# A layer input rearranged in DRAM ahead of the merge that reads it: a two-layer edge GNN with residual and layernorm

## The chip, the cores and the metric

The kernel runs on one core of a Trainium2 chip. The metric is the device time of one execution in microseconds (us); the kernel before is given by the median of three runs. All times of single instructions come from one profiled execution.

## The reference

There are 100,000 nodes with 96 features (`x`) and 50,000 edges, sorted by destination, with 32 features each. Two convolutions follow one another, and the result is added to the input and normalised:

```python
def conv(x, src, dst, edge_attr, W_msg, W_edge, W_root, b):
    msg = x[src] @ W_msg + edge_attr @ W_edge
    agg = segment_max(msg, dst, num_segments=x.shape[0])
    agg = where(isneginf(agg), 0.0, agg)
    return agg + x @ W_root + b
c1 = leaky_relu(conv(x, ..., layer 1))
c2 = leaky_relu(conv(c1, ..., layer 2))
out = layernorm(x + c2)          # over the 96 features, eps 1e-5
```

## The kernel before, in words

The work runs as four stages, one after the other: edge phase 0, merge 0, edge phase 1, merge 1 (called the first and second edge phase and the first and second merge below). The first two make layer 1, the last two layer 2 with the residual sum and the layernorm.

**Edge phase.** It loops over 98 groups of 512 edges (the last one shorter). GpSimd gathers the source rows with four indirect DMAs per group (L397). TensorE turns edges (L443), makes messages (L450), VectorE runs a segmented maximum as a scan (L866), and TensorE turns the result back (L460) so that VectorE can keep it in `hold`. Between the groups the node rows pass through TensorE for `x @ W_root + b` (L473, L482); ScalarE copies this "root" part out (L634) and stores it to DRAM in halves of superblocks (L638). Loads are issued by SP: edge attributes (L286), keep row (L294), node blocks (L266, L272). The rings hold four edge groups and four node units.

**Merge.** The nodes are cut into 49 superblocks of 2048 rows (the last has 1696), 16 blocks of 128 each; each superblock has two halves. A superblock's table in DRAM (`root`, `nodes_1`) is in superblock order: partition p holds rows p*16 to p*16+15 of the table, so that each partition reads one contiguous run; block j of partition p is node j*128+p of the superblock. SP loads the root part of a half (L313) into one of four buffers, ScalarE seeds it into PSUM (L670), TensorE adds the maxima with a one-hot matrix per chunk and block (L570, 1172 steps), and ScalarE evacuates the half (L684). In the first merge VectorE makes the one-hots (L880) and SP stores the half to `nodes_1` (L336). In the second merge GpSimd widens one-hot bytes that were stored earlier (L412, L430), and VectorE finishes each superblock: leaky relu (L932), add `x` (L935), statistics (L937), then the small steps of the variance (L945 to L951, with ScalarE's square root at L719), and the normalisation, 13 of 16 blocks on ScalarE (L725) and three on VectorE (L955). SP stores the result (L349).

**x in the second merge.** `load_x(s)` (L319 to L331) reads superblock s of `x` straight from the input. `x` is in node order, so partition p gets 16 rows that lie 128 rows apart: 2048 runs of 384 bytes. Two buffers `x_in` alternate; the load for s waits until VectorE has added the one for s - 2.

**SP's order.** SP issues its DMAs in one order written out by hand, each behind its own wait (L353 to L378). In the first merge it takes, half by half, the store of half h (waits for the evacuation) and the root load of half h + 8 (waits for the seed of half h + 4). After that it waits for the last stores (L360 to L363) and signals `ready` (L364), for which GpSimd waits before the gathers of the second edge phase (L407). In the second edge phase it takes a group's attributes, its keep row and the node blocks that are due. Before the second merge it issues two superblocks' root loads, the first two of x, and two more superblocks' root loads; in the merge, for each s, it loads x for s + 1, root for s + 4, and stores the output of s - 1.

Of the kernel before, what the change touches and what calls it, by code (L numbers as in the profile page):

```python
# [5 lines left out]
F32 = mybir.dt.float32  # L6
# [6 lines left out]
P = 128  # L13
# [3 lines left out]
DMA = 16  # L17
# [3 lines left out]
SBN = RI * P  # L21
# [19 lines left out]
def gnn(nc, x, src, dst, edge_attr, weights, out):  # L41
    N, D = x.shape
# [6 lines left out]
    NE = EG + 1  # L49
    CH = -(-E // P)  # L50
    E_END = E - (CH - 1) * P
    NSB = -(-N // SBN)
    N_END = N - (NSB - 1) * SBN
# [15 lines left out]
    with ExitStack() as ctx:  # L69
        def sb(name, shape, dt):  # L70
            return ctx.enter_context(nc.sbuf_tensor(name, shape, dt))

        def sem(name):
            return ctx.enter_context(nc.semaphore(name))

        def sems(name, n=2):
            return [sem(f"{name}{i}") for i in range(n)]


        root = nc.dram_tensor("root", (NSB * SBN, D), F32, kind="Internal").ap()  # L80
        nodes_1 = nc.dram_tensor("nodes_1", (NSB * SBN, D), F32, kind="Internal").ap()
        keep_dram = nc.dram_tensor("keep_row", (E,), BF16, kind="Internal").ap()

        onehot_dram = nc.dram_tensor("onehot_bytes", (-(-NBATCH // 2), P, 2 * BATCH * P), U8, kind="Internal").ap()

        def table(a, s):
            return a[s * SBN:(s + 1) * SBN, :].rearrange("(p j) d -> p (j d)", j=RI)

        def unit_of(a, u):
            s, h = divmod(u, 2)  # L90
            return table(a, s)[:, h * UB * D:(h + 1) * UB * D]
# [15 lines left out]
        rows = sb("rows", [ROWS_ON + 1, TP], I32)  # L107
# [18 lines left out]
        x_in = [arena[:, UNIT_RING * UW + (3 + i) * SW:UNIT_RING * UW + (4 + i) * SW] for i in range(2)]  # L126
# [60 lines left out]
        bytes_stored, bytes_in = sems("bytes_stored"), sems("bytes_in")  # L187
        stepped, seeded, evacuated = sems("stepped"), sems("seeded"), sems("evacuated")
        root_back, nodes_stored = sems("root_back", UNIT_RING), sems("nodes_stored", 3)
        x_back, vec_2, var_done, dev_done, norm_set = sems("x_back"), sem("vec_2"), sem("var_done"), sem("dev_done"), sem("norm_set")  # L190
        norm_a, norm_v, out_stored = sem("norm_a"), sem("norm_v"), sems("out_stored", 3)


# [16 lines left out]
        def byte_batches(g):  # L210

            span = NE - BYTES_AT
            return range((g - BYTES_AT) * NBATCH // span, (g + 1 - BYTES_AT) * NBATCH // span) if g >= BYTES_AT else range(0)
# [14 lines left out]
        def unit_uses(u, layer):  # L228
            return uses(u, UNIT_RING, NU, layer)
# [2 lines left out]

        X_ADDED, X_ADD = 4, 2
        LAST_BLOCKS = -(-N_END // P)

        def scalar_blocks(s):

            return LAST_BLOCKS // 2 if s == NSB - 1 else 15 if s >= NSB - 3 else 13

# [6 lines left out]
        def _(sp):  # L246
            first = 8
            src_groups = src[0:EG * GE].rearrange("(g p r) -> p g r", p=P, r=C)
            to = src_all[:, 0:EG * C].rearrange("p (g r) -> p g r", r=C)
# [11 lines left out]
            def load_nodes(layer, u):  # L261
                if u >= UNIT_RING:
                    sp.wait_ge(nt_full, layer * NG + (u - UNIT_RING + 1) * UG)
                to = node_in[u % UNIT_RING]
                if layer:
                    sp.dma_start(to, unit_of(nodes_1, u)).then_inc(block_in[u % UNIT_RING], DMA)  # L266
                    return
                rows = U_END if u == NU - 1 else UN
                full = rows // GE
                to = to.rearrange("p (q j d) -> p q j d", j=C, d=D)  # L270
                at = x[u * UN:u * UN + full * GE, :].rearrange("(q p j) d -> p q j d", p=P, j=C)
                sp.dma_start(to[:, 0:full, :, :], at).then_inc(block_in[u % UNIT_RING], DMA)  # L272
                if rows > full * GE:
                    at = x[u * UN + full * GE:N, :].rearrange("(p j) d -> p j d", j=C)
                    sp.dma_start(to[0:(rows - full * GE) // C, full, :, :], at).then_inc(block_in[u % UNIT_RING], DMA)

            def store_bytes(k):
                sp.wait_ge(bytes_made, k + 1)
                sp.dma_start(onehot_dram[k // 2][:, k % 2 * BW:(k % 2 + 1) * BW], bytes_out[:, k % 2, :]).then_inc(bytes_stored[k % 2], DMA)

            def edge_phase(layer):
                for g in range(NE):
                    t = EdgeGroup(layer, g)
                    if t.o >= EDGE_RING:
                        sp.wait_ge(turned, max(t.o - EDGE_RING + 1, layer * NE))
                    sp.dma_start(gathered[t.ring][0:t.p, :, D:K], attr_at(t)).then_inc(attr_in[t.ring], DMA)  # L286
                    if t.o == 0:
                        sp.wait_ge(keep_made, 1)
                        sp.dma_start(keep_dram.rearrange("(p c) -> p c", c=MC), keep_all).then_inc(keep_stored, DMA)
                        sp.wait_ge(keep_stored, DMA)  # L290
                    if t.o >= EDGE_RING:
                        sp.wait_ge(scanned, t.o - EDGE_RING + 1)
                    row = keep_dram[g * GE:g * GE + t.cols].rearrange("(a e) -> a e", a=1)
                    sp.dma_start(keep[0:D, t.ring, 0:t.cols], row.broadcast_to([D, t.cols])).then_inc(keep_in[t.ring], DMA)  # L294
                    for u in unit_loads.get((layer, g), ()):
                        load_nodes(layer, u)
                    if layer == 0:
                        for k in byte_batches(g - EDGE_RING):
                            store_bytes(k)
                for u in unit_loads.get((layer, NE), ()):  # L300
                    load_nodes(layer, u)
                if layer == 0:
                    for g in range(NE - EDGE_RING, NE):
                        for k in byte_batches(g):
                            store_bytes(k)

            def load_root(layer, u):
                if u >= UNIT_RING:
                    sp.wait_ge(seeded[layer], (u - UNIT_RING + 1) * UG)
                else:  # L310
                    sp.wait_ge(nt_full, (layer + 1) * NG)
                sp.wait_ge(root_stored[u % UNIT_RING], DMA * unit_uses(u, layer))
                sp.dma_start(root_in[u % UNIT_RING], unit_of(root, u)).then_inc(root_back[u % UNIT_RING], DMA)  # L313

            def load_roots(layer, s):
                for u in (2 * s, 2 * s + 1):
                    load_root(layer, u)

            def load_x(s):  # L319
                if s >= 2:  # L320
                    sp.wait_ge(vec_2, X_ADDED * (s - 2) + X_ADD)
                else:
                    sp.wait_ge(eb_full, 2 * NE)
                    sp.wait_ge(no_full, 2 * NG)
                rows = N_END if s == NSB - 1 else SBN
                full = rows // P
                to = x_in[s % 2].rearrange("p (j d) -> p j d", d=D)
                at = x[s * SBN:s * SBN + full * P, :].rearrange("(j p) d -> p j d", p=P)
                sp.dma_start(to[:, 0:full, :], at).then_inc(x_back[s % 2], DMA)
                if rows > full * P:  # L330
                    sp.dma_start(to[0:rows - full * P, full, :], x[s * SBN + full * P:N, :]).then_inc(x_back[s % 2], DMA)  # L331

            def store_half(h):
                s, at = h // 2, slice(h % 2 * HG * C * D, (h % 2 + 1) * HG * C * D)
                sp.wait_ge(evacuated[0], (h + 1) * HG)
                sp.dma_start(table(nodes_1, s)[:, at], nodes_out[s % 3][:, at]).then_inc(nodes_stored[s % 3], DMA)  # L336
# [19 lines left out]
            for h in range(2 * NSB):  # L356
                store_half(h)
                if h + 8 < NU:
                    load_root(0, h + 8)
            for k in range(3):  # L360
                sp.wait_ge(nodes_stored[k], 2 * DMA * ((NSB + 2 - k) // 3))
            for i in range(2):
# [2 lines left out]
            edge_phase(1)  # L365
            load_roots(1, 0)
            load_roots(1, 1)
            load_x(0)
            load_x(1)
            load_roots(1, 2)  # L370
# [364 lines left out]
        def _(dve):  # L735
# [133 lines left out]
            def hold_chunks(t):  # L869
                dve.wait_ge(eb_full, t.o + 1)  # L870
                whole = sum(n == P for _, n in t.chunks)
                a = t.g * C
                last = nc.vector.tensor_copy(hold[:, a:a + whole, :], eb_ps[:, 0:whole * D].rearrange("p (c d) -> p c d", d=D))
                for c, n in t.chunks[whole:]:
                    last = nc.vector.tensor_copy(hold[0:n, a + c, :], eb_ps[0:n, c * D:(c + 1) * D])
                last.then_inc(held, 1)
# [44 lines left out]
            def finish(s):  # L921
                blocks = LAST_BLOCKS if s == NSB - 1 else RI
                y = nodes_out[s % 3][:, 0:blocks * D]
# [68 lines left out]
```

## Time and profile before

| what | value |
|---|---|
| median of three runs | 1887.03 us (1883.07 to 1889.02) |
| span of the profiled execution, first to last instruction | 1876.7 us |
| time of the profiled execution itself | not listed apart from its span; the median lies 10.3 us above the span |
| busy: TensorE matmul / VectorE / ScalarE / GpSimd | 1519.6 / 1313.2 / 1080.4 / 1084.8 us |
| moved by DMA | 459.13 MB, 245 GB/s over the span |
| chain that ended last | TensorE 30%, VectorE 25%, DMA 19%, GpSimd 15%, issue 9% |
| mean granted TensorE clock | 0.950 |

How to read it: PE is TensorE's matmul, PEld its weight load, DVE is VectorE, ACT ScalarE, POOL GpSimd, SP SyncE; "SPq" is SP's instruction queue, and q1, q10 and q0 are the DMA queues of SP, ScalarE and GpSimd. L12 is line 12 of the kernel. The DMA share is the mean busy share of the core's 16 DMA engines. In the chain, "issue" is time in which an engine waited for nothing that the profile shows. A long fp32 matmul step at L570 stands as two matmul records. The busy shares are averages over four stages with different limits, so they say little by themselves.

### The profile page before, as it was taken

To read this page: it belongs to the slowest core of one execution; us is meant where nothing else is said; L and a number is where in the kernel's file an instruction comes from. 1 tells how busy PE (TensorE), PEld (TensorE's weight loads), DVE (VectorE), ACT (ScalarE), POOL (GpSimd) and SP (SyncE) were. 2 spreads that over 40 slices of the span, in tenths; PEclk is the share of its full clock that TensorE was granted. 3 is DMA by queue.
4 is the path that set the end of the run, shared out by engine and by line. 5 is a ranking of instruction groups with operands and counts; after the bars stand their busy time and mean duration, and the time that the engine had idled before them with its cause. 6 is when DMAs were issued, how large, how long until landed. Compare 5 with 4: busy or idle time off the path is not lost.

```text
span 1876.7 us, 37108 instructions
## 1 busy us (share of the span) xinstructions
PE 1519.6 (81%) x11422; PEld 1348.9 (72%) x11422; DVE 1313.2 (70%) x2383; ACT 1080.4 (58%) x2450; POOL 1084.8 (58%) x1454
## 2 busy tenths in 40 slices
PE   3998888988889888886889888988987767676763
PEld 3677777777778888885778777777777667666662
DVE  3677676777665555553667767677736899999998
ACT  2354444545443455553555555555535888888887
POOL 6777777767600000002777777777757787675663
PEclk9999999999999999998999999999998998988887
DMA  7779999999865777885788888888867899999996
GB/s 145 203 213 266 271 266 263 264 276 273 245 226 169 226 248 261 279 277 189 204 225 228 238 229 235 226 223 242 223 223 215 267 290 298 296 299 296 294 300 176
DMA packets 505022, 459.13 MB, mean 245 GB/s; under 512 B 348553, under 2 KB 412340, under 8 KB 504836
## 3 DMA queue, kind: packets, MB, share of 16 engines
q1 hardware_dynamic: 444118, 321.15, 59.9%
q0 software_dynamic: 30976, 57.72, 12.7%
q10 hardware_dynamic: 29742, 77.88, 10.6%
q8 instruction: 103, 1.69, 0.4%
q14 instruction: 83, 0.68, 0.1%
HBM read 283.25 MB, written 173.37 MB: 243 GB/s over the span
## 4 chain that ended last, share of the span: by engine, by line
PE 30%; DVE 25%; DMA 19%; POOL 15%; issue 9%; ACT 1%; SPq 1%; POOLq 0%; DVEq 0%; ACTq 0%
PE ps L570 18%; DMA onehot_bytes<-arena 14%; POOL arena L397 13%; DVE stats L937 6%; DVE arena L880 4%; DMA arena<-nodes,src_perm 4%; DVE arena L935 4%; DVE arena L932 4%; PE ps L482 4%; POOL onehot L430 2%; PE ps L450 2%; PE ps L473 2%; PE ps L443 2%; DVE arena L955 2%; DVE arena L866 1%
## 5 line engine op out<-in xcount | busy, mean ns | idle before, releaser
L570 PE MATMUL ps<-hold,onehot 128*128 x4688 | 612.7, 293 | 186.2 <-POOL onehot L430 139.5
L570 PEld LDWEIGHTS ps<-hold,onehot 128*128 128x128 f32 x4688 | 582.3, 205 | 217.0 <-issue 216.8
L397 POOL DMA_INDIRECT arena<-nodes,src_perm x392 | 370.0, 944 | 473.4 <-SPq L364 354.2
L482 PEld LDWEIGHTS ps<-w_root,onehot 97*128 97x128 f32 x3136 | 400.9, 194 | 99.7 <-issue 97.5
L397 POOL DMA_INDIRECT arena<-in_x_dram,src_all x392 | 374.4, 955 | 143.0 <-issue 114.3
L482 PE MATMUL ps<-w_root,onehot 97*128 97x128 f32 x3136 | 417.6, 277 | 0.0
L430 POOL CAST onehot<-keep 128x256 f32<-128x256 uint8 x588 | 298.8, 556 | 115.5 <-PE ps L570 72.4
L634 ACT COPY arena<-ps 128x384 f32<-128x384 f32 x392 | 187.5, 478 | 274.2 <-PE ps L482 272.4
L684 ACT COPY arena<-ps 128x384 f32<-128x384 f32 x392 | 166.6, 477 | 208.6 <-PE ps L570 208.5
L866 DVE TENSOR_TENSOR_SCAN arena<-keep,arena,ps 96x512 f32<-96x512 bf16 x196 | 247.7, 1264 | 46.6 <-PE ps L450 46.2
L880 DVE TENSOR_TENSOR onehot<-count,rel 128x1024 f32<-128x1024 bf16 x147 | 179.5, 1222 | 142.3 <-PE ps L570 141.2
L880 DVE TENSOR_TENSOR arena<-ps,rel 128x1024 uint8<-128x1024 f32 x147 | 175.5, 1216 | 110.6 <-DMA onehot_bytes<-arena 110.4
L473 PE MATMUL ps<-ident,arena 128*96 128x128 f32 x1568 | 240.9, 277 | 0.0
L725 ACT ACTIVATE arena<-arena,small 128x96 f32<-128x96 f32 x635 | 232.7, 454 | 1.6 <-DVE small L951 1.6
L450 PE MATMUL ps<-arena,w_edge 128*96 128x512 f32 x392 | 207.2, 611 | 0.0
L443 PE MATMUL ps<-ident,arena 128*128 128x128 f32 (+1 forms) x784 | 125.7, 284 | 96.2 <-DMA arena<-nodes,src_perm 63.7
L670 ACT COPY ps<-arena 128x384 f32<-128x384 f32 x392 | 175.9, 488 | 8.8 <-DMA arena<-root 8.3
L473 PEld LDWEIGHTS ps<-ident,arena 128*96 128x96 f32 x1568 | 177.2, 128 | 2.8 <-issue 2.4
L851 DVE TENSOR_TENSOR arena<-ps,arena 128x512 f32<-128x512 f32 x98 | 67.6, 690 | 146.9 <-ACT arena L613 144.5
L443 PEld LDWEIGHTS ps<-ident,arena 128*128 128x128 f32 (+1 forms) x784 | 93.2, 146 | 106.9 <-DMA arena<-nodes,src_perm 61.4
L624 ACT COPY onehot<-ps 96x512 f32<-96x512 f32 x196 | 114.3, 583 | 95.1 <-PE ps L473 92.4
L460 PE MATMUL ps<-ident,arena 96*128 96x96 f32 (+1 forms) x782 | 99.0, 249 | 52.8 <-DVE arena L880 51.8
(97 smaller groups left out, 1158.4 us busy)
## 6 DMA issues: line engine op xcount, KB each, us to landing
root<-arena ACTq DMA_DIRECT2D x196, 384.0 KB
arena<-root SPq DMA_DIRECT2D x196, 384.0 KB, 4.4
nodes<-arena SPq DMA_DIRECT2D x98, 384.0 KB, 2.7
arena<-nodes SPq DMA_DIRECT2D x98, 384.0 KB
arena<-in_x_dram SPq DMA_DIRECT2D x97, 384.0 KB
arena<-in_x_dram SPq DMA_DIRECT2D x48, 768.0 KB, 8.0
out_dram<-arena SPq DMA_DIRECT2D x48, 768.0 KB, 4.6
onehot_bytes<-arena SPq DMA_DIRECT2D x147, 128.0 KB
```

Of the source, the lines that this page charges most:

```text
L397: nc.gpsimd.indirect_dma_start(out=gathered[t.ring][0:t.p, i, 0:D], out_offset=None, in_=table_in, in_offset=bass.IndirectOffsetOnAxis(ap= ...
L430: last = nc.gpsimd.tensor_copy(onehot[:, k % NS, i:i + PIECE, :].rearrange("p t n -> p (t n)"), bytes_back(k, 1)[:, 0, i * P:(i + PIECE) * P])
L443: last = nc.tensor.transpose(et_ps[:, r:t.cols:C], gathered[t.ring][0:t.p, r, :], ident[0:t.p, 0:t.p])
L450: nc.tensor.matmul(em_ps[t.b2][0:D, 0:t.cols], w_edge[:, t.layer, :], edges_t[t.b2][:, 0:t.cols], start=True, stop=True).then_inc(em_full, 1)
L473: last = nc.tensor.transpose(nt_ps[m % 2][0:D, to], node_in[u % UNIT_RING][:, at:at + D], ident[:])
L482: last = nc.tensor.matmul(no_ps[m % 2][:, i * P:(i + 1) * P], nodes_t[m % NODE_RING][0:D + 1, i * P:(i + 1) * P], w_root[0:D + 1, layer * ...
L570: nc.tensor.matmul(ps_bytes[:, bass.ds(place_at, SLOT)].bitcast(F32), onehot[:, k % NS, i, :], flat[:, bass.ds(chunk_at, P)], start=False, ...
L634: nc.scalar.copy(root_out[u % UNIT_RING][:, at:at + C * D].rearrange("p (j d) -> p j d", d=D), no_ps[m % 2].rearrange("p (j k) -> p j k", ...
L670: nc.scalar.copy(slot[:, n % RING, :, 0:D], root_in[u % UNIT_RING][:, at:at + C * D].rearrange("p (j d) -> p j d", d=D),).then_inc(seeded[ ...
L725: last = nc.scalar.activation(nodes_out[s % 3][:, at], nodes_out[s % 3][:, at], ACT.Identity, bias=small[:, 5 + 2 * (s % 2), j:j + 1], sca ...
L866: nc.vector.tensor_tensor_scan(msgs[t.b2][0:D, at], keep[0:D, t.ring, at], em_ps[t.b2][0:D, at], msgs[1 - t.b2][0:D, GE - 1:GE], ALU.min, ...
L880: return nc.vector.tensor_tensor(to[:, 0:n, :], row.rearrange("p (a n) -> p a n", a=1).broadcast_to([P, n, P]), rel[:, k * BATCH:k * BATCH ...
```

## The change

A new DRAM table `x_laid` holds `x` in superblock order. It is filled by DRAM to DRAM transfers (`lay_x`), 25 of them in the first merge, after every fourth half, and 24 in the second edge phase, in every fourth group; each moves one superblock of 768 KB (the last one in two pieces). All are issued by SP and count on one semaphore, `laid`; SP waits for all of it before the first load of x in the second merge. `load_x` then reads `x_laid`, 128 runs of 6144 bytes. Engine work is as before.

```diff
+        x_laid = nc.dram_tensor("x_laid", (NSB * SBN, D), F32, kind="Internal").ap()
...
+        LAY_EVERY = 4
+        LAID_FIRST = NSB - NE // LAY_EVERY
...
                     for u in unit_loads.get((layer, g), ()):
                         load_nodes(layer, u)
+                    if layer and g % LAY_EVERY == 1 and LAID_FIRST + g // LAY_EVERY < NSB:
+                        lay_x(LAID_FIRST + g // LAY_EVERY)
...
+            def lay_x(s):
+                rows = N_END if s == NSB - 1 else SBN
+                full = rows // P
+                to = table(x_laid, s).rearrange("p (j d) -> p j d", d=D)
+                at = x[s * SBN:s * SBN + full * P, :].rearrange("(j p) d -> p j d", p=P)
+                sp.dma_start(to[:, 0:full, :], at).then_inc(laid, DMA)
+                if rows > full * P:
+                    sp.dma_start(to[0:rows - full * P, full, :], x[s * SBN + full * P:N, :]).then_inc(laid, DMA)
...
             def load_x(s):
...
-                to = x_in[s % 2].rearrange("p (j d) -> p j d", d=D)
-                at = x[s * SBN:s * SBN + full * P, :].rearrange("(j p) d -> p j d", p=P)
-                sp.dma_start(to[:, 0:full, :], at).then_inc(x_back[s % 2], DMA)
+                sp.dma_start(x_in[s % 2][:, 0:full * D], table(x_laid, s)[:, 0:full * D]).then_inc(x_back[s % 2], DMA)
                 if rows > full * P:
-                    sp.dma_start(to[0:rows - full * P, full, :], x[s * SBN + full * P:N, :]).then_inc(x_back[s % 2], DMA)
+                    at = slice(full * D, (full + 1) * D)
+                    sp.dma_start(x_in[s % 2][0:rows - full * P, at], table(x_laid, s)[0:rows - full * P, at]).then_inc(x_back[s % 2], DMA)
...
                 store_half(h)
                 if h + 8 < NU:
                     load_root(0, h + 8)
+                if h % LAY_EVERY == 1 and h // LAY_EVERY < LAID_FIRST:
+                    lay_x(h // LAY_EVERY)
...
             load_roots(1, 0)
             load_roots(1, 1)
+            sp.wait_ge(laid, DMA * (NSB + (1 if N_END % P else 0)))
             load_x(0)
             load_x(1)
```

## Rows read from the trace of the kernel before

**Rows 1.** Windows by stage: busy us by engine, granted clock, DMA share, GB/s
```profile
core 0: us, PE busy (x) PEld busy (x) DVE busy (x) ACT busy (x) POOL busy (x), PEclk, DMA share, GB/s
...
549.00:871.00 322.00, 282.36 (x2344) 268.81 (x2344) 178.39 (x148) 160.61 (x389) 0.00 (x0) 0.99 0.73 239
871.00:1377.00 506.00, 440.85 (x3327) 378.84 (x3328) 350.50 (x493) 264.93 (x491) 371.16 (x394) 0.97 0.81 223
...
1500.00:1830.00 330.00, 225.91 (x1564) 214.38 (x1563) 307.76 (x974) 292.38 (x793) 227.99 (x441) 0.87 0.99 296
```

**Rows 2.** The chain of waits, 1500 to 1830 us, by line
```profile
by line: DVE stats L937 28.8%; DVE arena L935 20.3%; DVE arena L932 20.1%; DVE arena L955 7.9%; issue 5.5%; ACT small L719 3.4%; DVE small L951 3.2%; DVE small L950 2.9%; DVE small L948 2.7%; DVE small L945 2.6%; DVE small L947 2.0%; DVE sm
```

**Rows 3.** Who waited for whom, 1500 to 1830 us (us in total, times, longest)
```profile
DVE small L950 <- ACT small L719: 13.5, 36, 0.4
```

**Rows 4.** A VectorE group, 1500 to 1830 us (busy us, mean ns, idle)
```profile
L932 DVE SCALAR_TENSOR_TENSOR arena<-arena 128x1536 f32<-128x1536 f32 x37 | 68.9, 1863 | 0.0
```

**Rows 5.** The chain of waits, 560 to 840 us, by line
```profile
by line: PE ps L570 87.6%; issue 12.4%
```

**Rows 6.** Chain of waits, 900 to 1370 us, and one piece
```profile
by line: POOL arena L397 44.2%; DMA arena<-nodes,src_perm 15.8%; issue 14.9%; PE ps L482 9.5%; PE ps L450 5.1%; PE ps L473 4.8%; PE ps L443 4.1%; PE ps L460 1.8%
...
1252.58 7.55 DMA arena<-nodes,src_perm
```

**Rows 7.** Line L397 alone, 900 to 1370 us: ns, and idle before
```profile
L397 POOL DMA_INDIRECT arena<-nodes,src_perm x372: 929/944/957, 899.3 to 1362.5; - x186
...
  issue: 107.6, 353
  PE ps L443: 5.8, 19
```

**Rows 8.** Queue q10, 900 to 1370 us (packets, MB, share), and issues
```profile
q10 hardware_dynamic: 13413, 36.64, 19.7%
...
root<-arena ACTq DMA_DIRECT2D x94, 384.0 KB
```

**Rows 9.** Queue q1, 1500 to 1830 us, and issues (us to landing last)
```profile
q1 hardware_dynamic: 158751, 84.39, 86.2%
...
out_dram<-arena SPq DMA_DIRECT2D x36, 768.0 KB, 4.8
arena<-in_x_dram SPq DMA_DIRECT2D x36, 768.0 KB, 8.0
arena<-root SPq DMA_DIRECT2D x72, 384.0 KB, 6.1
```

**Rows 10.** Line L329 alone, whole span: time of SP's issue, ns min/median/max
```profile
L329 SPq DMA_DIRECT2D arena<-in_x_dram x49: 384/1874/5982, 1378.7 to 1850.4; - x49
```

**Rows 11.** Waits of ScalarE, 1377 to 1877 us
```profile
ACT ps L670 <- DMA arena<-root: 3.5, 3, 1.4
```

**Rows 12.** DMA queue q1 and the root loads, 560 to 840 us
```profile
q1 hardware_dynamic: 24473, 66.85, 73.8%
...
arena<-root SPq DMA_DIRECT2D x86, 384.0 KB, 3.6
```

**Rows 13.** Waits of ScalarE, 549 to 871 us
```profile
ACT ps L670 <- DMA arena<-root: 2.8, 3, 1.3
```

**Rows 14.** Waits of SP, 560 to 840 us
```profile
SPq L336 <- ACT arena L684: 184.1, 86, 9.7
SPq L313 <- ACT ps L670: 33.1, 85, 0.4
```

**Rows 15.** Windows of 40 us, columns as in Rows 1
```profile
560.00:600.00 40.00, 36.38 (x307) 34.70 (x306) 22.88 (x19) 13.24 (x32) 0.00 (x0) 1.00 0.45 146
...
640.00:680.00 40.00, 34.50 (x288) 32.83 (x288) 22.30 (x19) 19.85 (x48) 0.00 (x0) 1.00 0.75 239
...
760.00:800.00 40.00, 35.09 (x295) 33.42 (x295) 22.30 (x19) 23.16 (x56) 0.00 (x0) 1.00 0.87 278
```

**Rows 16.** The chain of waits, 868 to 878 us, one piece
```profile
871.66 2.29 DMA nodes<-arena
```

**Rows 17.** Waits of SP, 900 to 1370 us
```profile
SPq L294 <- DVE arena L866: 309.8, 90, 6.7
```

More of the change, by code:

```diff
@@ L189, in gnn @@
         root_back, nodes_stored = sems("root_back", UNIT_RING), sems("nodes_stored", 3)
-        x_back, vec_2, var_done, dev_done, norm_set = sems("x_back"), sem("vec_2"), sem("var_done"), sem("dev_done"), sem("norm_set")
+        x_back, laid, vec_2, var_done, dev_done, norm_set = sems("x_back"), sem("laid"), sem("vec_2"), sem("var_done"), sem("dev_done"), sem("norm_set")
         norm_a, norm_v, out_stored = sem("norm_a"), sem("norm_v"), sems("out_stored", 3)
```

## The prediction

> **What bounds the kernel now.** I read the stages first, then in each stage the chain of waits, then the DMA queues. The windows by stage [rows 1] show three that the change touches: the first merge (549 to 871 us), the second edge phase (871 to 1377) and the second merge (1377 to the end). The reader should see that the DMA engines are at 0.99 only from 1500 to 1830 us, the stage that is to read x in long runs, and that the other two stages have 0.73 and 0.81 in use.
>
> A full DMA share is not yet a bound. The chain in 1500 to 1830 us [rows 2] runs over VectorE lines (L937, L935, L932, L955) and names no transfer. VectorE is busy 307.8 of 330 us [rows 1] and its only listed wait is 13.5 us for the square root of ScalarE [rows 3]; it never waits for x. It passes L932, once per superblock and 1.86 us long, 37 times in the 330 us [rows 4]: a period of about 9.1 us. In the first merge the chain is TensorE at L570 (87.6%) and "issue" between its pieces (12.4%) [rows 5]. In the second edge phase it is mostly GpSimd's gather, 944 ns each with 0.3 us between (107.6 us over 353) [rows 6, 7]: 1.25 us each, 5.0 us for a group of four.
>
> **Prices.** A long packet: the root stores of the second edge phase are alone on q10, 94 of 128 packets of 3072 bytes in 19.7% of 16 x 470 us = 1481 us [rows 8], so 123 ns each and 0.98 us of all 16 engines for 384 KB. A short packet: q1 takes 86.2% of 16 x 330 = 4551 us [rows 9]; its 72 root loads are 72 x 128 x 0.123 = 1134 us, and 3417 us are left for 36 x loads and 36 out stores of 2048 runs of 384 bytes, 23.2 ns each, 2.97 us of all engines for 768 KB. An x load by 128 runs of 6144 bytes, at the pace of long packets, costs 2 x 0.98 = 1.96 us. So the second merge saves 1.0 us of DMA per superblock, 49 us in all.
>
> **What the second merge gains: 1 us.** VectorE's chain hides the x load before and after: a load is issued after L935 of the superblock before last, lands 8.0 us later [rows 9], and is wanted two periods (18 us) after. Nothing waits, so nothing goes. SP's issue of an x load takes 1.87 us in the median and up to 5.98 [rows 10] and will drop, but SP then waits for ScalarE anyway. At the stage's start ScalarE waits 3.5 us for root [rows 11], partly beside the first two x loads: I take -1, between -3.5 and 0.
>
> **What the lay-out costs.** 49 transfers of 2048 runs (one more small one for the tail): 25 in the first merge, one after every fourth half superblock, and 24 in the second edge phase, one in every fourth group. The trace has no DRAM to DRAM transfer. Its read half is the x load's, 2.97 us, and its write half the out store's, 2.97 us. If both overlap it costs 2.97 us of all engines, if they follow each other 5.94. No row lies nearer to one end, so I take the middle, 4.5; DMA time below nothing is excluded. The Trainium skill, in "DMA: Bandwidth & Descriptors" (Latency and other measured facts), gives 207 to 214 GB/s per direction for copies between HBM tensors with 16 KiB rows, which would make 3.7 us as an estimate from that page; the transfer would then fit more easily than at 4.5. No run here shows it.
>
> Out stores write runs of 384 bytes to DRAM and land in 4.8 us, where x loads reading such runs need 8.0 [rows 9]: the short write is not the slow side. Against that the Trainium skill says, in "DMA: Bandwidth & Descriptors" (Specifications), that transfers under 512 bytes lose line rate through a read-modify-write. By that rule the write half would be the dear one and the price nearer the upper end; the landing times don't bear it out.
>
> *First merge.* Its 98 stores and 98 root loads need 196 x 0.98 = 192 us of the 322, though the share is 0.73, 235 us: packets are stretched there (q1 has 73.8% of 16 x 280 us = 3306 us for 86 root loads and as many stores, 22,016 long packets, 150 ns per packet instead of 123 [rows 12]). With 25 lay-outs the need is 192 + 74, 112 or 149 = 266, 304 or 341 us, so it fits at the middle price. Latency: root for a half is loaded four halves ahead, 4 x 322/98 = 13.1 us; less about 2 us until seeding frees the buffer and 3.6 us of landing [rows 12], 7.5 us are left, and a lay-out ahead in the same queue takes at most 5.94. Root waits are 2.8 us now [rows 13]; I take +1, up to +4. SP waits 184.1 + 33.1 of 280 us here [rows 14], so an issue of 0.4 to 6 us is covered, though it pushes the following store and root load back inside the same slack.
> TensorE's own pace: x307 matmuls in 40 us at DMA share 0.45, x288 at 0.75 and x295 at 0.87 [rows 15]. For 2344 matmuls that is 305 against 318 us: 12 us for 0.42 more share if it is a slope, nothing if it has levelled off, as the two later windows say. The share would rise by 0.23 to 0.46. I take +4, between 0 and +13.
>
> *Between the stages.* The last lay-out (h = 97) is issued between the last store and the signal "ready", for which GpSimd's gathers wait. The store lands in 2.29 us [rows 16]; an issue of 1.87 us hides under it, one of 5.98 adds 3.7. Then the first edge and node loads stand behind a lay-out. Taken: +0.5, up to +3.7.
>
> *Second edge phase.* 410 us busy + 71, 108 or 143 = 481, 518 or 553 of 506. Again the busy time contains stretched packets, so I expect it to fit. GpSimd's pace needs no transfer: a ring of four groups is 20 us; less 5 us of its own issue, 7.5 us of landing (row at 1252.58 [rows 6]) and about 1 us of turning, 6 us are free, and a lay-out delays by 4.5 in the middle. GpSimd waits 5.8 us for the ring now [rows 7]. Key rows, edge attributes and node blocks are loaded three to four groups ahead, and SP has 309.8 us of waiting there [rows 17]. If this cover fails TensorE starves group by group. I take +2, from 0 to +8. The new wait on "laid" stands before load_x(0); behind it are load_x(1) and root loads 4 to 7, for which ScalarE would wait. The last lay-out is issued at group 93, some 20 us before, so it costs 0.
>
> **Sum:** -1 + 1 + 4 + 0.5 + 2 = +6.5 us. The profiled execution has a span of 1876.7 us, 10.3 below the median of 1887.0; its own whole time is not listed, so I carry the difference over unchanged: 1893.5.
>
> **The rivals.** (1) *All hidden.* TensorE's pace has levelled off and every queue has its slack: 1886 to 1888. For it: the last two windows of [rows 15], and GpSimd's fixed 1.25 us. Chance 0.18. (2) *The DMA engines become the bound* where there was room. If stretched packets are real need, the middle price overruns both stages: 235 + 112 - 322 = 25 and 518 - 506 = 12, 1924 in all; at the upper price 62 + 47, 1996. It decides from 3.5 us per lay-out on in the first merge (87/25). Against it: packets of the same size take 123 ns on q10, and at share 0.99 nobody waits for x. 0.15. (3) *Faster:* the full DMA share does hold the second merge, through VectorE. Of 330 us there, 307.8 + 13.5 are work and the square root; only 8.7 can go, x 49/36 = 12 us, and 3.5 at the start, less some 4 for the lay-outs: 1876. It decides if those 8.7 us are late transfers; against it, the chain puts 5.5% (18 us) on "issue" between dependent instructions [rows 2], which no transfer shortens. 0.10. (4) *The long runs are not there:* the loads of the laid-out table still go as short packets, or SP's issue stays long. Then the costs stay and the -1 goes: 1894.5. 0.07.
>
> **How the numbers follow.** The forecast, a small loss of 2 to 15 us, has 0.50. A measurement of this kernel can tell about 0.3%, 5.7 us. Over that: 0.30 of the forecast's 0.50, rival 2, 0.05 of rival 4: 0.50. Within: 0.20 of the forecast, 0.15 of rival 1, 0.02 of rival 4: 0.37. Faster: rival 3 and 0.03 of rival 1: 0.13. The range goes from 1880, which takes in rival 1 and part of 3, to 1932, which takes in rival 2 at the middle price; about 0.15 stays outside.
>
> **What would show it.** In the profile after, windows of 0.9 to 1.0 DMA share in the first merge and edge phase and about 0.88 from 1500 to 1830; the second merge's length within 3 us of 500; packets under 512 bytes halved there and more by 100,000 (49 x 2048) before it; matmuls at L570 in pieces 4.4 to 4.5 us apart; ScalarE's wait on root in the first merge under 7 us. The forecast is wrong if VectorE's periods shrink below 9.0 us, if L397 waits for TensorE by tens of us, or if L670 waits for root by more than 15 us. Landing of the lay-outs, 8 us or 16, tells the price.

## The result and the profile after

The changed kernel takes 1898.07 us in the median of five runs (1893.4 to 1904.15), the kernel before 1887.03 in five beside it (1879.45 to 1889.02); the ratio is 1.0066, 95% interval 1.0042 to 1.0089. It is slower, by 11.0 us in the medians and 12.5 by the ratio. A second comparison of the same kernel gave 1.0087 (1.0053 to 1.0121): 1900.1 against 1881.57 us, 18.5 us in the medians and 16.4 by the ratio.

For the changed kernel both the time of the profiled execution (1896.51 us) and its span (1894.7 us) are known: 1.8 us lie around the span, not the 10.3 us that I had carried over. By the same 1.8 us the profiled execution of before took about 1878.5 us, an estimate, and was quicker than each of the five beside it. So the two traces differ by 18.0 us, more than the medians do, and a part of what they show is scatter between executions. The second profile and those of the experiments tell which part.

The stages of the changed kernel, in the windows view (columns as in [rows 1]):

```profile
550.00:883.00 333.00, 285.88 (x2343) 273.09 (x2344) 177.89 (x146) 160.30 (x387) 0.00 (x0) 0.98 0.88 287
883.00:1390.00 507.00, 439.65 (x3332) 378.68 (x3332) 350.17 (x493) 265.36 (x491) 371.19 (x394) 0.97 0.92 262
...
1512.00:1842.00 330.00, 226.30 (x1568) 214.43 (x1568) 303.26 (x958) 290.19 (x787) 236.00 (x436) 0.88 0.90 294
```

The DMA share rose from 0.73 to 0.88 and from 0.81 to 0.92 in the two stages that now lay x out, and fell from 0.99 to 0.90 in the one that reads it. VectorE is as good as fully busy there as before (303.3 against 307.8 of 330 us): the relief bought nothing. By stage, in us, from the start times of the instructions at L570, L397 and L932 of before and their successors (a superblock counts as finished when VectorE starts its last steps at L932):

| profile | first merge, first to last matmul | second edge phase, first to last gather | second merge, finished superblock 1 to 13 | 13 to 41 |
|---|---|---|---|---|
| before | 321.5 | 488.2 | 130.3 | 256.5 |
| changed | 333.5 | 488.2 | 132.3 | 259.8 |
| changed, second profile | 340.8 | 488.2 | 138.3 | 255.3 |

About two thirds of what the traces differ by is in the first merge (12.0 of 18.0 us, and 19.3 of 27.8 in the second profile); the second edge phase carries its 24 lay-outs for nothing.

**Where the first merge loses.** Windows of 40 us of the changed kernel; set against [rows 15] (x307, x288, x295 matmuls in 40 us):

```profile
560.00:600.00 40.00, 36.36 (x307) 34.69 (x306) 22.46 (x20) 13.25 (x32) 0.00 (x0) 1.00 0.59 181
...
680.00:720.00 40.00, 34.17 (x288) 32.50 (x286) 22.72 (x19) 21.53 (x52) 0.00 (x0) 1.00 0.97 322
...
760.00:800.00 40.00, 33.38 (x268) 31.90 (x268) 20.12 (x18) 21.53 (x52) 0.00 (x0) 0.96 0.95 315
800.00:840.00 40.00, 33.37 (x271) 32.07 (x270) 20.63 (x17) 21.53 (x52) 0.00 (x0) 0.96 0.96 315
```

At a DMA share of 0.97 TensorE kept its old pace (x288, as before from 680 to 720 us); at 0.95 it lost 9% (x268 where it was x295). The share is not what decides. The chain of waits of the changed kernel, 808 to 834 us (start, us, what), shows the loss itself:

```profile
812.90 3.85 PE ps L586 x32
...
816.84 1.24 DVE onehot L896
818.08 1.03 issue
819.11 9.04 PE ps L586 x64
828.14 0.60 issue
828.75 3.83 PE ps L586 x32
```

TensorE stands still from 816.75 to 819.11 us. The chain names VectorE's one-hots, but those that TensorE needs next had been made at 816.3. What it waits for is its own load of the next sixteen step words (the places in the merge, read from SBUF into registers once per two batches), which runs from 815.7 to 818.9 us. From the timeline and from line L570 alone (PEldq is TensorE's instruction queue):

```profile
815.05 1.23 DVE L896 TENSOR_TENSOR onehot<-count,rel 128x1024 f32<-128x1024 bf16 x1 [1.68 <-PE ps L586]
```

```profile
L570 PEldq TENSOR_LOAD <-rows x1: 3206/3206/3206, 815.7 to 815.7; - x1
```

All such loads of the first merge (ns min/median/max), before and then changed:

```profile
L554 PEldq TENSOR_LOAD <-rows x73: 862/1268/1870, 552.1 to 868.5; - x73
```

```profile
L570 PEldq TENSOR_LOAD <-rows x73: 862/1194/4308, 553.0 to 881.1; - x73
```

The median is no worse, the longest goes from 1.87 to 4.31 us. Added up over the merge (74 with the first one, which starts before it), the loads take 96.8 us before and 105.3 after, 8.5 more; five of them last over 2 us (3.05, 2.47, 3.28, 3.21 and 4.31). All five overlap lay-out packets, where 27 of all 74 loads do. TensorE's gaps between matmuls (those over 150 ns) grow by as much, from 39.0 to 47.1 us. SP's queue shows in the timeline what stood around the load of 815.7 us, a lay-out and a store whose issue was held for 2.89 us:

```profile
811.44 0.55 SPq L329 DMA_DIRECT2D x_laid<-in_x_dram  x1
...
812.57 2.89 SPq L349 DMA_DIRECT2D nodes<-arena  x1
```

The second part is TensorE's clock. Windows of the changed kernel before and after the gap:

```profile
809.00:816.70 7.70, 6.84 (x60) 6.50 (x58) 3.83 (x4) 4.97 (x12) 0.00 (x0) 1.00 1.03 321
819.00:828.00 9.00, 8.89 (x64) 8.85 (x64) 3.67 (x3) 4.97 (x12) 0.00 (x0) 0.81 0.75 249
```

Having stood for 2.4 us, TensorE works part of the next 9 us at the lower of its two levels (granted clock 0.81 where it was 1.00): 64 matmuls take 9.04 us, where two pieces of 32 take 7.66. This happens after three gaps (2.5, 2.4 and 3.6 us; pieces at 794.23, 819.11, 859.26), 1.38 us each, and not after one of 2.3 us (720.68). In the second profile it follows four of six gaps of 2.6 to 3.2 us, so not every such stop costs it. 8.5 + 3 x 1.38 = 12.6 us, against 12.0 measured for the stage.

What I had feared did not come. ScalarE's waits for root, 2.8 us before [rows 13], and q1 with its root loads (us to landing last) in the changed kernel's first merge:

```profile
ACT ps L686 <- DMA arena<-root: 2.5, 3, 1.0
```

```profile
q1 hardware_dynamic: 67915, 83.64, 88.7%
...
arena<-root SPq DMA_DIRECT2D x86, 384.0 KB, 4.4
```

**The second merge** (1512 to 1842 us), to be set against [rows 9] and [rows 3]: q1 fell from 86.2% to 77.9%, x lands in 7.0 instead of 8.0 us, and VectorE's only listed wait is still the one for ScalarE's square root. That wait grew from 13.5 to 18.2 us (longest 3.0), which is more than the 3.3 us that the steady part of the stage lost in this profile.

```profile
q1 hardware_dynamic: 87815, 83.61, 77.9%
...
arena<-x_laid SPq DMA_DIRECT2D x36, 768.0 KB, 7.0
```

```profile
DVE small L966 <- ACT small L735: 18.2, 35, 3.0
```

### The profile page after: what moved, and what is told of

Read it like the earlier page. It is cut to its first block, busy times and chain, and to the rows that moved or that the text cites. A ratio compares the mean times of both kernels' runs of the same rounds, so it can differ in the third digit from the quotient of the medians.

```text
span 1894.7 us, 37158 instructions
## 1 busy us (share of the span) xinstructions
PE 1526.6 (81%) x11422; PEld 1359.2 (72%) x11422; DVE 1310.3 (69%) x2383; ACT 1081.1 (57%) x2450; POOL 1091.4 (58%) x1454
## 4 chain that ended last, share of the span: by engine, by line
PE 31%; DVE 20%; DMA 19%; POOL 18%; issue 10%; SPq 1%; ACT 1%; DVEq 0%; ACTq 0%; POOLq 0%
PE ps L586 20%; POOL arena L413 14%; DMA onehot_bytes<-arena 13%; DVE stats L953 4%; POOL onehot L446 4%; DVE arena L896 4%; DMA arena<-nodes,src_perm 4%; PE ps L498 4%; DVE arena L951 3%; DVE arena L948 3%; PE ps L489 2%; PE ps L466 2%; PE ps L459 1%; DVE arena L882 1%; DVE arena L971 1%
## 5 line engine op out<-in xcount | busy, mean ns | idle before, releaser
L586 PE MATMUL ps<-hold,onehot 128*128 x4688 | 622.4, 296 | 193.8 <-POOL onehot L446 135.9
L586 PEld LDWEIGHTS ps<-hold,onehot 128*128 128x128 f32 x4688 | 592.2, 208 | 224.2 <-issue 224.0
L446 POOL CAST onehot<-keep 128x256 f32<-128x256 uint8 x588 | 305.1, 569 | 114.2 <-PE ps L586 75.6
```

The source lines that it names most:

```text
L446: last = nc.gpsimd.tensor_copy(onehot[:, k % NS, i:i + PIECE, :].rearrange("p t n -> p (t n)"), bytes_back(k, 1)[:, 0, i * P:(i + PIECE) * P])
L586: nc.tensor.matmul(ps_bytes[:, bass.ds(place_at, SLOT)].bitcast(F32), onehot[:, k % NS, i, :], flat[:, bass.ds(chunk_at, P)], start=False, ...
```

## The experiments

Theory A: the loss is in the first merge, where lay-outs hold up TensorE's loads of step words and the clock falls after the long gaps; the rest is scatter. Rivals put part of it into the second merge (B), into chance (C), or held that full DMA engines do bound something (D). Stage times in us, one profile each, as in the table above:

| run | ratio, 95% interval | first merge | second edge phase | superblocks 1 to 13 | 13 to 41 |
|---|---|---|---|---|---|
| lay_merge_only | 1.0094 (1.0062 to 1.0126) | 341.5 | 488.1 | 131.0 | 258.1 |
| lay_edge_only | 1.0013 (0.9993 to 1.0033) | 322.4 | 488.2 | 130.8 | 256.0 |
| long_runs_only | 1.0017 (0.999 to 1.0045) | 321.3 | 489.2 | 139.7 | 256.1 |
| lay_both_edges | 1.0434 (1.0405 to 1.0462) | 323.3 | 489.1 | 141.6 | 256.3 |
| lay_halves | 1.0039 (1.0019 to 1.0059) | 326.6 | 488.2 | 130.1 | 256.2 |
| lay_merge_act | 1.0078 (1.0051 to 1.0104) | 332.8 | 488.2 | 128.6 | 255.6 |
| lay_both_edges_act | 1.0282 (1.0252 to 1.0312) | 321.7 | 488.1 | 135.1 | 255.8 |
| words4 | 1.0464 (1.0433 to 1.0495) | 362.7 | 488.9 | 148.8 | 287.1 |
| long_runs_3072 | 1.0001 (0.9985 to 1.0018) | 322.3 | 488.5 | 129.7 | 257.6 |
| lay_second_edge_all | 1.0015 (0.999 to 1.0041) | 321.4 | 488.6 | 130.2 | 259.5 |
| lay_merge_double | 1.0185 (1.0154 to 1.0215) | 355.1 | 488.2 | 130.8 | 256.2 |
| changed_again | 1.0087 (1.0053 to 1.0121) | 340.8 | 488.2 | 138.3 | 255.3 |

### The parts one by one

**Lay-outs in the first merge alone** (against the changed kernel):

```diff
-                    if layer and g % LAY_EVERY == 1 and LAID_FIRST + g // LAY_EVERY < NSB:
-                        lay_x(LAID_FIRST + g // LAY_EVERY)
...
-                sp.dma_start(x_in[s % 2][:, 0:full * D], table(x_laid, s)[:, 0:full * D]).then_inc(x_back[s % 2], DMA)
+                sp.dma_start(to[:, 0:full, :], at).then_inc(x_back[s % 2], DMA)
```

> The 25 lay-outs of the first merge stay, the 24 of the second edge phase are left out, and x is read from the input in short runs as before. Theory A (the loss is in the first merge: TensorE's loads of step words are held up by the lay-outs, and its clock falls after the long gaps): first merge about 333 us instead of 321, the rest as before, ratio to the kernel before 1.005 to 1.007. Rival B (part of the loss is in the second merge, where the traces differ by 6 us, because of the long runs): ratio 1.002 to 1.004. Rival C (the two profiled executions differ mostly by chance): ratio within 1.002.

These 25 lay-outs carry the whole loss and more, beyond the 333 us and the 1.007 that theory A had named: first merge 341.5 us, ten step-word loads over 2 us, all ten beside lay-out packets (31 of the 74 loads are). B and C fall as explanations of the whole.

**Lay-outs in the second edge phase alone** (the same with `lay_x` left out of the first merge instead):

> The 24 lay-outs of the second edge phase stay, those of the first merge are left out, and x is read from the input as before. Theory A: the gathers set the pace, so the second edge phase stays at 488 us from first to last gather and the ratio is 0.999 to 1.001. A rival by which DMA load costs wherever it stands: +6 us or more, ratio over 1.003.

As theory A has it: 488.2 us, and a ratio that can't be told from 1.

**Long runs alone**:

```diff
+                if s < NSB - 1:
+                    sp.dma_start(x_in[s % 2][:, 0:full * D], table(x, s)[:, 0:full * D]).then_inc(x_back[s % 2], DMA)
+                    return
```

> No lay-outs; the second merge reads x by runs of 6144 bytes straight from the input (all superblocks but the last), so the residual adds x rows in the wrong order. This is the change's gain without its cost. Theory A: VectorE's chain hides the loads, second merge unchanged within 2 us, DMA share 0.90 instead of 0.99, ratio 0.998 to 1.001. Rival B: slower by about 6 us, ratio 1.003. Rival D (the full DMA share did hold the second merge): faster by 8 us or more, ratio under 0.996.

No gain: D falls. B's ratio of 1.003 lies inside the interval, so a small loss by the long runs is not excluded. The steady part of the second merge is untouched (256.1 us), but superblocks 1 to 13 took 139.7 us instead of 130.3, which theory A had not said and B had; see the runs of 3072 bytes below.

### All lay-outs in the edge phases

```diff
-                if h % LAY_EVERY == 1 and h // LAY_EVERY < LAID_FIRST:
-                    lay_x(h // LAY_EVERY)
...
-                    if layer and g % LAY_EVERY == 1 and LAID_FIRST + g // LAY_EVERY < NSB:
-                        lay_x(LAID_FIRST + g // LAY_EVERY)
+                    if g % LAY_EVERY == 1 and (LAID_FIRST + g // LAY_EVERY < NSB if layer else g // LAY_EVERY < LAID_FIRST):
+                        lay_x(LAID_FIRST * layer + g // LAY_EVERY)
```

> The 25 lay-outs move from the first merge into the first edge phase, one in every fourth group; everything else is as in the changed kernel. Theory A: the first merge returns to 321 us; the first edge phase already has a DMA share of 0.86 and TensorE waits there on VectorE's bytes, so it pays between 0 and 6 us; ratio 0.999 to 1.003. If the cost of a lay-out follows from the DMA share alone, the first edge phase, fuller than the first merge, pays 12 us or more: ratio over 1.006.

I was far off: the first merge is back at 323 us, but it begins at 625.3 us instead of 549.1. The first edge phase lost 76 us, over six times the 12 of the rival. The waits of this kernel, 20 to 620 us, and line L282 alone, the byte stores (ns of SP's issue, min/median/max):

```profile
DVE arena L894 <- DMA onehot_bytes<-arena: 146.2, 52, 6.8
...
PE ps L474 <- DVE arena L894: 98.2, 32, 6.3
```

```profile
L282 SPq DMA_DIRECT2D onehot_bytes<-arena x147: 319/320/5244, 114.4 to 619.1; - x147
```

There a loop is closed over a transfer: VectorE makes one-hot bytes into two buffers, waits until the store of the last but one has landed (110.4 us in all before, 146.2 now), and TensorE waits for VectorE (51.8 us before, 98.2 now). A lay-out ahead of the store in SP's queue can lengthen a round. Part of the 76 us is TensorE's clock: from 20 us to just before the merge (620 us here, 540 before) its granted clock is 0.90 where it was 0.98, and its busy time 490 us where it was 456. With the 25 lay-outs of that phase issued by ScalarE, in its own edge phase after its root stores:

```diff
+                    if layer == 0 and g % LAY_EVERY == 1:
+                        lay_x(g // LAY_EVERY)
```

> As the run with all lay-outs in the two edge phases, which lost 76 us in the first one, but ScalarE issues the 25 of the first edge phase (q10). Theory Q: the 76 us come from VectorE's byte stores standing behind lay-outs in SP's queue (VectorE waits for a store with only two buffers); in another queue the stores pass, and the first edge phase falls from 625 to 550 to 570 us, ratio 1.000 to 1.012. Theory L (DMA load as such): it stays at 600 us or more, ratio over 1.03.

It begins the merge at 592.6 us: 33 of the 76 us went with the place in the queue, 43 stay. VectorE's waits for the byte stores are 131.6 us and TensorE's for VectorE 73.5, still above those of before, and the granted clock is 0.94. That the rest comes from stores sharing the engines with lay-outs is likely, not shown. The truth lies between both theories, and nearer to L than I thought.

### What makes the step-word loads long

**The grain.** Each lay-out cut in two, issued after every second half:

```diff
+                js = slice(c * RI // 2, (c + 1) * RI // 2)
+                sp.dma_start(to[:, js, :], at[:, js, :]).then_inc(laid, DMA)
...
-                if h % LAY_EVERY == 1 and h // LAY_EVERY < LAID_FIRST:
+                if h % 2 == 1 and h // 2 < 2 * LAID_FIRST - 1:
```

> As the run with lay-outs in the first merge alone (first merge 341.5 us, ratio 1.009), but each lay-out is cut into two of 1024 runs, issued after every second half; the same bytes and as many packets. Theory A1 (a step-word load of TensorE is late because it falls into a long burst of lay-out packets and the backlog behind it): bursts are half as long, no load over 2.5 us, first merge 321 to 328 us, ratio under 1.004. Theory A2 (the amount of DMA work decides, not its grain): first merge 335 to 345 us as with whole lay-outs, ratio 1.007 to 1.012.

A1: two loads over 2 us instead of ten, the longest 2.32, and 326.6 us instead of 341.5, for nearly the same bytes (49 halves instead of 50) at a higher DMA share (0.91 instead of 0.86 from 560 to 850 us). The intervals of the two ratios do not touch.

**The queue.** The lay-outs issued by ScalarE after every fourth half:

```diff
                     reseed(2 * s + 1)
+                    if layer == 0 and s % 2 == 0:
+                        lay_x(s // 2)
```

> As the run with lay-outs in the first merge alone, but ScalarE issues them, so they stand in q10 and not ahead of SP's stores and root loads in q1. If the long step-word loads come from the backlog in SP's queue: none over 2 us, first merge near 322 us. If from the DMA engines being full, whichever queue fills them: 335 to 345 us, as before. ScalarE's own issue costs 0.6 us each, hidden by its waits on TensorE.

332.8 us, short of the 335 to 345 of the second theory but far from 322. In this kernel's profile eleven loads last over 2 us, none over 2.44 (line of the load, ns min/median/max):

```profile
L559 PEldq TENSOR_LOAD <-rows x74: 846/1331/2441, 551.3 to 884.3; - x74
```

This fits loads of 3 to 4 us by the backlog in SP's queue and those just over 2 by the filled engines, but one run that also moves the lay-outs in time does not show it; and seven of its gaps, 10.2 us, ended with VectorE's one-hots and not with the load. This run also gives a lay-out's price, since in 560 to 850 us the lay-outs are alone in q10:

```profile
q10 hardware_dynamic: 43293, 16.50, 21.2%
...
x_laid<-in_x_dram ACTq DMA_DIRECT2D x21, 768.0 KB, 7.8
```

21.2% of 16 x 290 us = 984 us over 21 x 2048 packets is 22.9 ns each, 2.93 us of all engines per superblock: the lower end of my range, as the landing after 7.8 us says too. Reading and writing overlap, and 384-byte runs at both ends in DRAM cost what they cost at one end (23.2 ns). 786,432 bytes in 2.93 us of engine time would be 268 GB/s each way. The Trainium skill gives 207 to 214 GB/s per direction for copies between HBM tensors ("DMA: Bandwidth & Descriptors", Latency and other measured facts); that is a rate of whole copies, and no run here made such copies alone, so the two can't be set against each other. The Trainium skill also says there, under Specifications, that transfers under 512 bytes fall below line rate by a read-modify-write. The first half agrees: 384 bytes in 22.9 ns are 16.8 GB/s per engine, 3072 bytes in 123 ns are 25.0. A dearer write side is not seen.

**The dose.** 49 lay-outs in the first merge:

```diff
-                if h % LAY_EVERY == 1 and h // LAY_EVERY < LAID_FIRST:
-                    lay_x(h // LAY_EVERY)
+                if h % 2 == 1:
+                    lay_x(h // 2)
```

> 49 lay-outs in the first merge, after every second half, instead of 25; none in the second edge phase; x read as before. If the cost follows the need at unstretched prices, 192 + 49 x 2.95 = 337 us of DMA work stand against 321 us of TensorE time and the stage becomes DMA-bound: first merge 350 to 375 us, with ScalarE waiting for root loads. If a lay-out costs the same each as with 25 (12 to 20 us in 25): first merge 345 to 361 us without waits for root.

355.1 us, 33.6 more than before, with 7.7 us of ScalarE's waits for root; both of my cases had room for that time. The step-word loads add up to 128.2 us, 31.4 more, 18 of them over 2 us (16 beside lay-out packets). Even at a DMA share of 1.02 (560 to 850 us; the share adds up the packets' recorded times, so it can pass 1) the loss goes through these loads and not through a late transfer. The six first merges with lay-outs, against the kernel before (us more):

| run | first merge | step-word loads | gaps between matmuls | loads over 2 us, of them beside lay-out packets | all 74 loads: beside lay-out packets |
|---|---|---|---|---|---|
| changed | 12.0 | 8.5 | 8.1 | 5, 5 | 27 |
| changed_again | 19.3 | 13.1 | 12.9 | 8, 7 | 27 |
| lay_merge_only | 20.0 | 14.1 | 14.2 | 10, 10 | 31 |
| lay_halves | 5.1 | 3.7 | 4.4 | 2, 2 | 44 |
| lay_merge_act | 11.3 | 10.3 | 10.6 | 11, 10 | 36 |
| lay_merge_double | 33.6 | 31.4 | 28.1 | 18, 16 | 54 |

The loads and the gaps grow together. What the stage lost beyond the gaps is longer busy time of TensorE: 4 to 7 us in the four kernels in which its clock fell after gaps, under 1 us in the two in which it did not.

**Shorter loads.** The kernel before, without lay-outs:

```diff
-                    if k % 2 == 0:
-                        words = load_words(k * BATCH, min(2 * BATCH, TP - k * BATCH))
...
+                        if i % 4 == 0:
+                            words = load_words(k * BATCH + i, 4)
+                        word = words[i % 4]
```

> The kernel before, with TensorE's step words loaded four at a time, every fourth step, instead of sixteen at a time; no lay-outs. Theory A says that TensorE's idle gaps in the first merge (39 us in 73 gaps) are these loads (1.1 to 1.9 us each, partly hidden by queued matmuls). If a load of four is short enough to hide (under about 0.8 us), the first merge falls from 321 to 285 to 300 us and the ratio to 0.985 to 0.992; if a load costs 0.9 us whatever its size, four times as many make the merge longer, ratio over 1.01.

```profile
L554 PEldq TENSOR_LOAD <-rows x293: 327/333/878, 552.9 to 914.8; - x147
```

A load of four takes only 333 ns, and the gaps over 150 ns in the merge shrink from 39 to 23 us, yet the merge grows by 41 us: four times as many loads are 123.3 us in the queue instead of 96.8, and TensorE's recorded busy time for the same matmuls grows from 282 to 336 us. Most likely the loads now stand between matmuls that the queue then hands over late; the profile does not show it directly. Neither of my two cases came; the attempt to beat both kernels failed.

### The long reads, and a place that costs nothing

**Runs of 3072 bytes**, two per partition, otherwise as the run with long reads alone:

```diff
+                    for c in range(2):
+                        at = slice(c * UB * D, (c + 1) * UB * D)
+                        sp.dma_start(x_in[s % 2][:, at], table(x, s)[:, at]).then_inc(x_back[s % 2], DMA)
```

> As the run with long reads and no lay-outs (x rows added in the wrong order, all superblocks but the last), but each x load is cut into two of 128 runs of 3072 bytes. In the profiles so far the stretch from the first to the 13th finished superblock takes 128.6 to 131.0 us in five kernels that read x in short runs and 132.3 to 141.6 us in four that read runs of 6144 bytes, with a lower granted TensorE clock. If packets of 6144 bytes ahead of GpSimd's byte loads are the cause: 129 to 132 us here, ratio 0.998 to 1.001. If the cause is the clock falling by chance or the emptier DMA stage as such: 133 to 141 us again, ratio 1.001 to 1.004.

129.7 us for superblocks 1 to 13, ratio 1.0001. Windows of that stretch, of the long runs alone and then of this run:

```profile
1404.00:1543.00 139.00, 101.19 (x684) 96.22 (x684) 101.19 (x324) 95.15 (x255) 104.00 (x194) 0.84 0.73 232
```

```profile
1411.00:1541.00 130.00, 91.83 (x691) 86.54 (x690) 101.18 (x324) 96.00 (x259) 104.23 (x197) 0.93 0.80 250
```

The same matmuls, with a granted clock of 0.84 instead of 0.93. In that stretch TensorE and GpSimd wait for each other in turn. Six profiles with runs of 6144 bytes have 130.2 to 141.6 us there (mean 136.2), seven with shorter runs 128.6 to 131.0 (words4 left out). The one at 130.2 keeps me from calling it shown; it is likely worth some 5 us to the changed kernel.

**All 49 lay-outs in the second edge phase**, in every second group:

```diff
+                    if layer and g % 2 == 1:
+                        lay_x(g // 2)
```

> All 49 lay-outs stand in the second edge phase, one in every second group, none in the first merge; x is read in long runs of 6144 bytes. Theory A: the first merge is back at 321 us. GpSimd's gather rate sets the second edge phase; with 24 lay-outs more its busy DMA time would be about 0.92 + 0.14 of the stage, so it stays at 488 to 495 us if stretched packets give way, and ratio is 1.000 to 1.004 (the start of the second merge keeps its few us of loss). If 49 lay-outs fill the DMA engines beyond the stage's slack, gathers come late and it grows to 510 us or more: ratio over 1.011.

```profile
870.00:1378.00 508.00, 443.10 (x3333) 379.32 (x3332) 350.46 (x493) 266.26 (x492) 371.50 (x394) 0.97 1.01 299
```

```profile
POOL arena L411 <- issue: 107.6, 353, 0.3
```

The DMA engines are at 1.01 for 508 us, and the stage takes 488.6 us instead of 488.2: GpSimd issues its gathers at 1.25 us as before. This is the whole change without its loss, 1.0015 (0.999 to 1.0041), and still without a gain. No version beat the kernel before.

**The changed kernel again:**

> The changed kernel once more, for a second profile. Theory A: the first merge takes 330 to 342 us again, with several step-word loads over 2 us, each beside a lay-out; second edge phase 488 us. The 6 us that the first profile of the changed kernel shows in the second merge: if by chance, the second merge is within 2 us of the kernel before now; if from the long runs, 4 us or more longer again. Ratio 1.004 to 1.009.

340.8 us in the first merge, eight step-word loads over 2 us (seven beside lay-out packets), the longest 3.97. The steady part of the second merge, 3.3 us longer in the first profile, is 1.2 shorter here: that was chance. Superblocks 1 to 13 are 8.0 us longer than before, so over both parts the second merge is 6.8 us longer, which by the rule set beforehand speaks for the long runs.

## Why the prediction was right, and where it was not

Range and direction held: 1898.1 against 1893.5 (1880 to 1932), slower, and by 11 us within the 2 to 15 of the forecast; the second comparison (16.4 to 18.5 us) lies a little above it. The direction rested on the right stage but not on what happened there, and other terms were wrong in both directions, so the total owes something to luck. The terms:

- *The second merge gains nothing*: right, shown by the long runs alone. The -1 at its start became rather +2 to +8, likely by the long runs themselves; my text had bounded it at nothing above.
- *First merge, +1 for root and +4 for TensorE's pace*: the sum was mis-sized, 12.0 and 19.3 us in the two profiles. Root never became late (2.5 us), as the slack of 7.5 us said. I saw the "issue" gaps between pieces and asked whether they grow with the DMA share, by a slope or not at all. That step failed in kind: the gap is one load of words to registers, it grows in single jumps where a burst passes, and three of the long gaps cost 1.38 us of clock each besides. A mean over windows of 40 us could not show that; the line of the load (862/1268/1870) was there to be read.
- *The price of a lay-out*: 2.93 us where I took 4.5 between 2.97 and 5.94. Neither half was the dear one.
- *Between the stages, +0.5*: 4.3 instead of 3.8 us from the start of the last matmul to the first gather, +0.5.
- *Second edge phase, +2*: 0.0, and 0.4 with twice the lay-outs. The gather's pace hid everything, as its 6 us of slack said; the +2 was caution.
- *The time around the span*, carried over as 10.3 us: it is 1.8. The difference was the scatter of before, and it cancels in the forecast of the loss. Beside the later runs the medians of before were 1881.6 to 1882.7 us.
- Rival 1 (all hidden, 1886 to 1888) is excluded by the measured loss. Rival 2 (the DMA engines as the bound) was wrong in mechanism even where the share passed 1. Rival 3 (faster) was excluded by the long runs alone, rival 4 by the packets: the reads did become long, q1's busy share fell by 8 points.

Not shown: by which path a lay-out holds up a register load of TensorE. No load was moved away from the bursts while all else stayed.

## What to carry to other kernels

In this kernel a busy DMA share was no bound where no chain named a transfer, and work put into "free" DMA time was free only where the pace was set by something that no transfer delayed: 49 lay-outs cost nothing beside GpSimd's gathers, 25 cost 12 to 20 us beside TensorE's register loads and 76 us beside a two-buffer loop closed over a store. Read, for the stage that is to take the work, the longest duration of every small operation in its loop and not the mean, and look for a round trip with few buffers. If bulk transfers must go in, try them cut fine and spread out: in halves they cost 5 us here instead of 20.

## What the runs showed of the hardware that I had not expected

- A load of sixteen words from SBUF to TensorE's registers took 0.86 to 1.87 us in the first merge of the kernel before, up to 2.12 in other kernels without lay-outs there, and up to 4.31 beside bursts of 2048 packets of 384 bytes. In the second merge of the kernel before, where x itself is read in such bursts, four of 74 loads took over 2 us, the longest 2.65.
- After three stops of 2.4 to 3.6 us TensorE ran the next 64 matmuls in 9.04 instead of 7.66 us, with a granted clock of 0.81 from 819 to 828 us; after some other stops of that length, in the second profile, it did not.
- Copies from DRAM to DRAM by 384-byte runs cost 22.9 ns per packet, no more than loads and stores of such runs (23.2 ns, their mean).
- A DMA share of 1.01 over 508 us left a stage's time unchanged (488.6 against 488.2 us).
